# Two batches of attention share their tile shapes on TensorE, and row maxima are turned by a DMA that ScalarE issues

## The reference, cut to what matters

```python
def _mhsa(x, w_qkv, b_qkv, w_o, b_o):          # 8 heads of 64 channels
    t = x.reshape(B, C, H * W).transpose(0, 2, 1)
    q, k, v = jnp.split(t @ w_qkv + b_qkv, 3, axis=-1)
    q, k, v = (heads(q), heads(k), heads(v))
    scores = jnp.einsum('bhnd,bhmd->bhnm', q, k) / jnp.sqrt(jnp.float32(hd))
    attn = jax.nn.softmax(scores, axis=-1)
    out = jnp.einsum('bhnm,bhmd->bhnd', attn, v)
    return out.transpose(0, 2, 1, 3).reshape(B, H * W, C) @ w_o + b_o
...
hyp_out = _logmap0(_mhsa(_expmap0(x * m), hdn_w_qkv, ...))
euc_out = _mhsa(x * (1.0 - m), eu_w_qkv, ...)
return x + hyp_out + euc_out                    # x in the calls is _gn(x)
```

## Time and profile before

| | |
|---|---|
| median of 3 runs | 4022.13 us (4021.23 to 4025.07) |
| the profiled execution | 4021.88 us, its span 4020.2 us, mean granted clock 0.998 |
| busy, share of the span | PE 98%, PE weight loads 59%, DVE 58%, ACT 48%, POOL 66% |
| chain that ended last | PE 94%, DVE 2%, POOL 1%, DMA 1% |

### The profile page before, as it was taken

How to read it: one execution, slowest core, us unless ns; L and a number is a source line. 1 busy time by engine, 2 the same in 40 slices (tenths; PEclk the granted TensorE clock), 3 DMA queues, 4 the chain that set the end, 5 groups by cost and what they waited for, 6 DMA issues and landing times.

```text
span 4020.2 us, 57048 instructions
## 1 busy us (share of the span) xinstructions
PE 3937.1 (98%) x21664; PEld 2379.5 (59%) x21664; DVE 2345.5 (58%) x2553; ACT 1928.7 (48%) x3489; POOL 2664.2 (66%) x1303
## 2 busy tenths in 40 slices
PE   4999999999999999999999999999999999999998
PEld 3556566565655656556565665656556565565654
DVE  5464755647556475565746557465674656646455
ACT  4454534545345453555535545354553545535443
POOL 4584875838667486674857658675685756858468
PEclk9999999999999999999999999999999999999999
DMA  8212031121311213112141120411113121121101
GB/s 277 100 42 95 32 116 58 43 95 32 124 50 48 95 32 126 53 48 90 32 135 49 48 79 32 142 48 68 53 47 127 48 74 48 56 96 44 58 11 64
DMA packets 137548, 293.12 MB, mean 73 GB/s; under 512 B 16704, under 2 KB 28992, under 8 KB 127296
## 3 DMA queue, kind: packets, MB, share of 16 engines
q1 hardware_dynamic: 137280, 289.47, 21.2%
HBM read 239.09 MB, written 50.33 MB: 72 GB/s over the span
## 4 chain that ended last, share of the span: by engine, by line
PE 94%; DVE 2%; POOL 1%; DMA 1%; issue 1%; ACT 1%; SPq 0%; POOLq 0%; DVEq 0%; ACTq 0%
PE aux_ps L1310 32%; PE acc_ps L1422 23%; PE score_ps L1408 22%; PE aux_ps L1359 8%; PE score_ps L1310 4%; PE aux_ps L1432 3%; DVE mxp L1173 1%; PE aux_ps L1369 1%; POOL sums L673 1%; DMA w_split<-v_y 0%; DMA w_split<-w_o 0%; DMA xin<-in_x_dram 0%; PE aux_ps L1328 0%; PE aux_ps L1325 0%; POOL w_o L653 0%
## 5 line engine op out<-in xcount | busy, mean ns | idle before, releaser
L673 POOL TENSOR_TENSOR sums<-sums,probs 128x1024 f32<-128x1024 f32 x768 | 1835.4, 2390 | 736.9 <-ACT probs L850 682.6
L1173 DVE TENSOR_REDUCE mxp<-aux_ps 128x2 f32<-128x1024 f32 x1014 | 1241.7, 1225 | 1299.9 <-PE aux_ps L1359 1291.5
L850 ACT ACTIVATE probs<-score_ps 128x512 f32<-128x512 f32 x2048 | 1058.1, 602 | 658.7 <-PE score_ps L1408 648.0
L1422 PE MATMUL acc_ps<-probs,v_y 128*64 128x512 f32 x4096 | 991.9, 605 | 0.0
L1310 PE MATMUL aux_ps<-xs,w_qk 128*128 128x512 f32 x2976 | 804.7, 408 | 0.0
L1310 PEld LDWEIGHTS aux_ps<-xs,w_qk 128*128 128x128 f32 x2976 | 524.8, 188 | 374.3 <-issue 279.1
L673 POOL TENSOR_TENSOR sums<-probs 128x1024 f32<-128x1024 f32 x128 | 305.0, 2383 | 432.8 <-ACT probs L850 432.1
L1422 PEld LDWEIGHTS acc_ps<-probs,v_y 128*64 128x64 f32 x4096 | 248.2, 136 | 475.2 <-issue 245.2
L1359 PE MATMUL aux_ps<-k_hi,q_hi 64*128 64x512 f32 x2028 | 454.0, 443 | 18.7 <-DVE mxp L1173 16.1
L1235 DVE RECIPROCAL den<-den 128x256 f32<-128x256 f32 (+1 forms) x240 | 443.4, 1848 | 17.3 <-ACT den L861 17.3
L1408 PE MATMUL score_ps<-q_hi,k_hi 64*128 64x512 f32 x2048 | 407.9, 393 | 1.0 <-issue 1.0
(11 more groups left out here) (142 smaller groups left out, 3195.2 us busy)
## 6 DMA issues: line engine op xcount, KB each, us to landing
w_qk<-w_split SPq DMA_DIRECT2D x124, 512.0 KB, 4.2
xin<-in_x_dram SPq DMA_DIRECT2D x232, 256.0 KB, 3.3
w_o<-w_split SPq DMA_DIRECT2D x32, 1024.0 KB, 7.3
w_v<-w_split SPq DMA_DIRECT2D x30, 1024.0 KB, 5.9
v_y<-in_x_dram SPq DMA_DIRECT2D x72, 256.0 KB, 3.0
y<-v_y SPq DMA_DIRECT2D x64, 256.0 KB, 2.0
xin<-y SPq DMA_DIRECT2D x64, 256.0 KB, 2.9
out_dram<-v_y SPq DMA_DIRECT2D x64, 256.0 KB, 6.5
```

Of the source, the lines that this page charges most:

```text
L673: pool.tensor_tensor(sums[h][:, :], a, probs[:, g % SLOTS_P, :], ALU.add).then_inc(c_sum[h].sem, 1)
L850: act.activation(probs[:, n % SLOTS_P, token_half(u % 2)], score_ps[:, u % SCORE_BANKS, :], ACT.Exp, scale=SCALE).then_inc(c_exp.sem, 1)
L1173: dve.tensor_reduce(mxp[:, :, n, h], ps, AX.X, ALU.max).then_inc(c_free["D"].sem, 1)
L1422: last = nc.tensor.matmul(acc_ps[head(j), :], v_y[:, m, head(2 * p + j)], probs[:, n % SLOTS_P, token_half(j)], start=(m == 0), stop=(m == ...
```

## The change

Four things, besides renumbered waits for constants at the start:
- A projection is made whole, in one batch, always an even one (`QK_AT` is unchanged and even); of v, four tiles are made in batch 0 and four in batch 2. A gate tile goes between the two halves of such a projection.
- Probs x v is left out in even batches that have a projection; the odd batch does it for the batch before and for its own (`held`), with a due denominator between the two. The last two tiles fall in batch 31.
- The maxima are no longer turned on PE. DVE combines them in two halves (after slots 11 and 15), and ACT issues a DMA that stores a half to DRAM piece by piece (128 partitions x 8 values of 4 bytes) and, one batch later, a DMA that loads it as two rows of 512 into rows 0 and 64 of `q_max`. The load waits for the store to land; PE waits for the load before the first scores of each half. The identity matrix goes.
- In ACT's batch the denominator copy and `project` move to the end, behind these DMAs. On SP the load of `w_o` moves behind the chunks of the image.

```diff
+HALF_DONE = (11, 15)
+NEG_STORE, NEG_LOAD = (-3, -1), (-2, 0)
...
+def neg_at(b, what):
+    for h in range(2):
+        p, r = divmod(b - what[h], 8)
+        if r == 0 and 1 <= p <= PAIRS:
+            return p, h
+    return None
...
-    out = [("v", m) for m in (2 * b, 2 * b + 1) if m < NT]
+    out = [("v", m) for m in range(2 * b, 2 * b + 4) if b % 2 == 0 and m < NT]
     for p in range(2, PAIRS + 2):
-        for k in range(4):
-            done = min(8 * p + QK_AT[k], BATCHES)
-            first = done if (p, k) in ((PAIRS, 0), (PAIRS + 1, 3)) else done - 1
-            out += [("qk", p, k, part) for part in range(2) if b == (first, done)[part]]
+        out += [("qk", p, k) for k in range(4) if b == min(8 * p + QK_AT[k], BATCHES)]
     return out
...
+def held(i, t, b):
+    if projects(i, t, b - b % 2):
+        return (b - 1, b) if b % 2 else ()
+    return (b - 1, b) if b == BATCHES - 1 else (b - 1,) if b % 2 or not projects(i, t, b - 2) else ()
...
+            def store_neg(i, t, p, h):
+                n = 0 if i is None else 4 * t + p
+                act.wait_ge(c_mx.sem, c_mx.at(i, h + 1 if i is None else 2 * (n - 1) + h + 1))
+                if i is not None:
+                    act.wait_ge(c_neg[h].sem, c_neg[h].at(i, 16 * (n - 1)))
+                act.dma_start(max_dram[h].rearrange("j (n q) -> q (j n)", q=P),
+                              mxw[:, h, :, :].bitcast(F32).rearrange("p j n -> p (j n)")).then_inc(c_mst[h].sem, 16)
+            def load_neg(i, t, p, h):
+                act.wait_ge(c_mst[h].sem, c_mst[h].at(i, 16 if i is None else 16 * (4 * t + p)))
...
+                act.dma_start(q_max[0:HD + 1:HD, p % 2, token_half(h)].bitcast(F32), max_dram[h]).then_inc(c_neg[h].sem, 16)
...
 @@ ScalarE @@
                    for b in range(BATCHES):
                         for g in (2 * b, 2 * b + 1):
                             exps(g)
                         if phase_at(b, DRAIN) is not None:
                             drain(phase_at(b, DRAIN))
-                        if phase_at(b, DEN) is not None:
-                            den_copy(phase_at(b, DEN))
-                        if neg_pair(b) is not None and wanted(i, t, neg_pair(b)):
-                            neg_rows(i, t, neg_pair(b))
                         for j in HI_AT.get(b, ()):
                             if wanted(i, t, PAIRS):
                                 operand_hi(i, t, j)
-                        project(b)
...
                         operand_step(i, t, b)
+                        neg_turn(b)
+                        if phase_at(b, DEN) is not None:
+                            den_copy(phase_at(b, DEN))
+                        project(b)
...
@@ VectorE @@
+            def combine(i, t, p, h):
+                aux_read(dve, i, (t, "max", p, HALF_DONE[h]))
+                if i is not None:
+                    dve.wait_ge(c_mst[h].sem, c_mst[h].at(i, 16 * (4 * t + p - 1)))
+                dve.tensor_reduce(mxw[:, h, :, :], mxp[:, :, 4 * h:4 * h + 4, :], AX.X, ALU.max,
+                                  negate=True).then_inc(c_mx.sem, 1)
...
 @@ TensorE @@
                        scores(2 * b + 1)
                         if wanted(i, t, p1):
                             max_slot(i, t, p1, s1)
-                        if b:
-                            prob_v(2 * b - 2)
-                            prob_v(2 * b - 1)
-                        if phase_at(b, DEN) is not None:
-                            denominator(phase_at(b, DEN))
-                        if neg_pair(b) is not None and wanted(i, t, neg_pair(b)):
-                            neg_rows(i, t, neg_pair(b))
-                        if t == 0 and b in GATE_BATCH and followed(i):
-                            gate_tile(i, t, GATE_BATCH[b])
+                        for bb in held(i, t, b):
+                            prob_v(2 * bb)
+                            prob_v(2 * bb + 1)
+                            if phase_at(b, DEN) is not None and bb == b - 1:
+                                denominator(phase_at(b, DEN))
                         project(b)
-                    prob_v(TILES - 2)
-                    prob_v(TILES - 1)
```

More of the change, by code:

```diff
@@ L179, in aux_tiles @@
                 out += [((t, what, pp, k), "D", (first, first + 1))]
-        return out + neg(p) + maxima(p + 1, 0)
+        return out + maxima(PAIRS + 1, 0)
     out = []
@@ L187, in aux_tiles @@
             out += [((t, "den", phase_at(b, DEN)), "A", (1,))]
-        if neg_pair(b) is not None and wanted(i, t, neg_pair(b)):
-            out += neg(neg_pair(b))
         if t == 0 and b in GATE_BATCH and followed(i):
             out += [((t, GATE_BATCH[b]), "D", (0,))]
-        for f in projections(b):
+        for f in projections(b) if b < BATCHES else ():
             if f[0] == "v":
-                out += [((t,) + f, "A", (LAST_SCORE if f[1] % 2 else 1 if f[1] == 6 else 2,))]
-            elif f[3] and wanted(i, t, f[1]):
-                out += [((t,) + f[:3], "Q", (2,))]
+                out += [((t,) + f, "A", (LAST_SCORE if f[1] % 2 else 2,))]
+            elif wanted(i, t, f[1]):
+                out += [((t,) + f, "Q", (2,))]
     if wanted(i, t, PAIRS + 1):
@@ L334, in build @@
         c_mx = counted("max_made", 16, 2)
+        c_mst = [counted(f"max_stored{h}", 16 * 8, 16) for h in range(2)]
+        c_neg = [counted(f"max_rows_loaded{h}", 16 * 8, 16) for h in range(2)]
         c_score = counted("scores_made", NSC)
@@ L577, in _ @@
                         load_chunks(i, 1, "norm", range(4, 8), next_image)
+                    load_wide(w_o, t, 6, c_wo)
                     sp.wait_ge(c_aux.sem, c_aux.at(i, at(i, (t, "v", NT - 1))[1] + 1))
@@ L616, in _ @@
                 sp.wait_ge(c.sem, 17 + B * 128 - 16 * PAIRS + 16)
+            for c in (*c_mst, *c_neg):
+                sp.wait_ge(c.sem, 17 + B * 128 - 16)
             sp.wait_ge(c_wv.sem, 1 + B * 64 - 32)
@@ L784, in qk_hi @@
                                bias=bias_q[:, tt, what, pp:pp + 1]).then_inc(c_hi.sem, 1)
[L786 to L790, removed]
+            def store_neg(i, t, p, h):
[7 more added lines that the diff above has]
+                act.wait_ge(c_mst[h].sem, c_mst[h].at(i, 16 if i is None else 16 * (4 * t + p)))
+                last = TILES * t + 16 * (p - 2) + 8 * h + 8
+                if i is not None and (i or last > 0):
+                    act.wait_ge(c_score.sem, c_score.at(i, 2 * last))
+                act.dma_start(q_max[0:HD + 1:HD, p % 2, token_half(h)].bitcast(F32), max_dram[h]).then_inc(c_neg[h].sem, 16)
             def split_hi(n):
@@ L877, in project @@
                     def project(b):
-                        for f in made(b):
+                        for f in projections(b):
                             if f[0] == "v":
@@ L882, in project, with neg_turn @@
                                 qk_hi(i, t, f[1], f[2])
+                    def neg_turn(b):
+                        if b == 0 and t:
+                            load_neg(i, 0, PAIRS, 1)
+                        elif b == 0 and i:
+                            load_neg(i - 1, 1, PAIRS, 1)
+                        elif neg_at(b, NEG_LOAD) and wanted(i, t, neg_at(b, NEG_LOAD)[0]):
+                            load_neg(i, t, *neg_at(b, NEG_LOAD))
+                        if neg_at(b, NEG_STORE) and wanted(i, t, neg_at(b, NEG_STORE)[0]):
+                            store_neg(i, t, *neg_at(b, NEG_STORE))
                     for b in range(BATCHES):
@@ L1361, in max_slot @@
                 last.then_inc(c_aux.sem, 1)
-            def neg_rows(i, t, p):
-                pe.wait_ge(c_mx.sem, c_mx.at(i, 2 if t < 0 else 2 * (4 * t + p)))
-                for h in range(2):
-                    ps = bank_free(pe, i, (t, "neg", p, h))
-                    for n in range(4):
-                        last = nc.tensor.matmul(ps[0:HD + 1, n * P:(n + 1) * P], mxw[:, 4 * h + n:4 * h + n + HD + 1],
-                                                ident[:, :], start=True, stop=True)
-                    last.then_inc(c_aux.sem, 1)
             for g in GATES:
@@ L1453, in project @@
                     def project(b):
+                        gate = GATE_BATCH[b] if t == 0 and b in GATE_BATCH and followed(i) else None
                         for f in projections(b):
```

78 lines of the change are left out of this document (30 added, 48 removed).

## The result

The changed kernel was not 2.4% faster, as forecast (3924 us), but about 1% slower. Two of its four runs fell to a granted clock of 0.616 and 0.670 and took 5748 and 5305 us (the plain median of the four is 4687.65); their cause is open, and they are left out here. The other two took 4059.43 and 4070.32 us, the kernel before 4021.23 to 4025.07 beside them; ratio 1.0105 (95% interval 1.0087 to 1.0124). The profiled execution is the one of 4059.43 us, span 4057.7.

A forecast was written before the change was run, and what follows sets the result against it. The prediction took PE, busy 98% of the span, as the bound: 116 us saved on PE, less 15 for DVE and 3 for the start, is 98, so 3924 us from 4022; range 3898 to 3974 (8 in 10).

The forecast's parts named there:

- The store's landing: ACT's store of half the maxima to DRAM: lands in some 4 us, hidden, costs nothing; 13 kept for the range.
- rival A: Slow store holds ACT's load, high halves and exps: 110 places per microsecond, gain gone at 9.4 us; slower, chance 0.07.
- The cover: Between ACT's store and load: a landing up to 9 us is hidden, 8 for the second half.
- The page's rule: Skill page on DMA receipts and writes under 512 B: would mean a slow store; by the rows it costs nothing.
- Merges: Joined PE runs: two Q runs of 6 into 12 save 0.24 us, two V runs of 8 into 16 save 0.15.
- Rival C: On PE, joined runs gain nothing, only the turned maxima do: 30 us less 3, 3995 us; chance 0.04.
- The sum of 116 us: PE's list shortened by joined projections and probs x v and turned maxima, less new neighbours: 116 us, at worst 93.
- the turn: Turning row maxima by DMA takes 0.47 us net off PE each time, 63 times: 30 us.
- DVE, 15 us: Shorter even batches make PE wait for DVE to read max tiles: 15 us lost, bounds 0 and 64.
- Rival B: DVE makes PE wait for max tiles in nearly every fourth batch: 60 us instead of 15, 3969 us; chance 0.13.
- The start, 3 us: First maxima stored and loaded by DMA among 1 MB transfers before the first scores: 3 us lost, bounds -1 and 8.
- the worst neighbours: Q runs on PE behind a max tile instead of V: at worst 23 us less gain, giving 3945 us.

The follow-up runs named there:

- the two sets of runs: The changed kernel measured twice, unaltered: first mean 4064.9 us (ratio 1.0105), then once more beside the other experiments 3997.02 us (ratio 0.9939).
- the best kernel: Changed kernel with stores in 32-byte runs, loads gathering, and only the very first maxima turned on PE with the identity: 3900.62 us, ratio 0.9699.
- the two halves of the pairing: Against the kernel before, maxima turned on PE: only projections made whole, 4201.25 us; only probs x v paired (v by four tiles), 4202.96 us.
- the second and fourth experiment: Second: kernel before with only the turn by DMA, 4091.92 us. Fourth: changed kernel with each load one batch later, slow store kept, 3939.32 us.
- the repeat: The changed kernel, unaltered, measured once more on the same chip as other experiments: 3997.02 us, ratio 0.9939.

## Why the prediction was wrong, step by step

- **The store's landing, the step that failed.** "I take the row of the small pieces, some 4 us, so nothing": it took 10.3 to 11.0 in the median, 18.4 and 15.4 at the start. The row chosen was a load of small pieces from DRAM; no row of before showed small stores to it. Both ends were in the text (3.7 and 13), and the choice between them decided the sign. This was rival A, with a chance of 0.07 for "slower", far too low for an operation that no row showed, with a cover of 9 us inside its bounds; and the 13 us that were kept "for the range" are in none of its numbers (3898 to 3974). What rival A said of the place held: ACT's load holds the projections' rounding. Its price, 110 us for a microsecond, came near the 91 of the two sets of runs in part by luck, as said there. Its point of decision was a little early: 9.4 us, where the changed kernel at 10.3 is still 25 us faster than before.
- **The cover.** 9 us were worked out, some 10.8 found, and that is two errors that partly cancel. The store was issued 2.6 us into its odd batch (522.22 with the first max tile at 519.61; 2.6 is also the median of the 126 later stores), not 5.0: in the timeline the issue stands before the batch's last exp. But the deadline wasn't the exps' 6.95 + 5.49 + 1.47 + 1.5 less 1.3 = 14.1. PE's second max tile comes sooner, at 6.95 + 5.49 + 0.43 + 1.84 = 14.7, less 0.7 for the rounding, 0.5 for the load's issue and 0.1 for semaphores: 13.4. 13.4 - 2.6 = 10.8 us are an estimate from these rows; the landing shown had 10.9. Without the denominator it is 0.86 less.
- **The clock.** The prediction counted a wait as its length. After the longer ones PE also worked at 1.2 GHz: 41 us of the 142 by which the changed kernel's span exceeds the one with 32-byte stores are PE's busy time, with the mean granted clock at 0.989 and 0.996. By these means the clock makes some 29 of the 41 (4057.7 x 0.011 - 3915.3 x 0.004, an estimate); the rest isn't traced.
- **The page's rule.** "DMA: Bandwidth & Descriptors" of the Trainium skill (Anatomy of one DMA, written for DMAs that GpSimd issues) warned of a surprisingly long delay of the receipt when the target is HBM; its Specifications say that below 512 B a DMA does read-modify-write. The runs agree with the first, for a DMA that ScalarE issued: the store is slow after its data have moved, below. But the second rule doesn't separate the cases: pieces of 32 B land in 1.4 us and pieces of 4 B, 64 B apart, in 2.7, all of them far under 512 B. The same page's Rules for kernel authors advise to make the last dimension contiguous. The edit that repaired it does so for the store, and undoes it for the load; spacing the values 64 B apart, against that advice, did nearly as well.
- **Merges.** Q 2.95 to 2.96 (2.96 forecast), V 3.58 to 3.59 (3.59), V with denominator 1.87 + 0.86 + 1.72 = 4.45 (4.45). Right. Rival C is out.
- **The sum of 116 us.** With the store repaired and the start as before, the kernel gains 4021.78 - 3900.62 = 121.2. Right within 5 us. How near it came is in part luck, since its parts sit less well. Alone, the turn gave 21 of 30 us. In the pairs it gave 3956.14 - 3900.62 = 55.5, most of it, as I read it, because there the turn stood inside a joined V run: 63 x (0.63 + 0.15) = 49. And the new order without it gave 66 where 86 less 63 x 0.15 = 77 were to be had; the missing 11 aren't explained.
- **DVE, 15 us.** Wrong, though harmless: in the best kernel PE waits for max tiles 10.9 us in 21 waits, in the one before 16.1 in 26. Rival B is out. But the mechanism is real, as the two halves of the pairing show: it bites at batches of 4.1 to 4.4 us, hardly at 5.49.
- **The start, 3 us.** Mis-sized. With 32-byte stores it costs 3916.77 - 3900.62 = 16.2 us in the total, 8.1 of them before the first probs x v. PE's waits for max tiles over the span are 10.3 us longer as well (21.2 against 10.9), I don't know why; with the changed kernel's own, 25.3 (138.9 - 113.6). I had counted 3.7 us for a landing; in the crowded start even the quick store takes 7.18 and its load 8.56, and the slow one 18.36.
- **The result put together.** 4064.9 - 3900.6 = 164 us stand between the best version and the changed kernel: 25 at the start, 139 at some 126 later landings, 1.1 us for each on average, waits and lower clock together.
- **A slip.** The upper end of the forecast's own range adds 23 us for the worst neighbours to 3924, which makes 3947 and not 3945; nothing hangs on it.

What stays open: the 11 us of the new order, and the 9 that the turn alone lacks in place.

## What to carry to other kernels

An operation that no row of the profile shows, placed ahead of others on an engine in order, is to be given the chance that its bounds have, not that of the nearest row: compare its cover (here 9 to 11 us) with both ends before the sum is made. A transposing store of single values to DRAM should be made contiguous on the DRAM side, and the load should do the gathering; and the wait for it belongs as late in the in-order engine's list as its reader allows. When batches are shortened by moving work to their neighbours, look at the shortest batch that results: what counts is whether every engine that frees banks still gets through in it.

## What the runs showed of the hardware

**The time of such a store passes after its data have moved.** The DMA view of 521 to 536 us of the changed kernel, 40 slices of 0.375 us (busy tenths of the DMA engines):

```profile
DMA  0000027200000000000000000000000000000106
```

The store issued at 522.22 keeps the engines busy from slice 6 to 8, until 524.0; it lands at 533.81. For 9.8 us nothing moves that the profile shows. Values 64 bytes apart land about four times sooner, though the queue moves more packets in all (264448 against 133632, since the load gathers too).

**Such a landing isn't steady** from one set of runs to another: 0.7 us in the median for the same kernel (11.0 and 10.3; 10.2 and 10.1 for the same store in the second and fourth experiment), with 0.6% faster in one set and 1% slower in the other, while the medians of the kernel before in the four sets lie within 0.02% (4021.78 to 4022.31). A kernel whose path holds such a landing can't be judged by one set.

**Small pieces cost much less when they are read than when they are written side by side**: the load that gathers 1024 values of 4 bytes lands in 4.8 us (my median from the semaphores' records), the store of as many in 10 to 11; 64 bytes apart the store took 2.7 to 3.5, less than the load.

**PE's granted clock falls after some of its longer waits.** 0.50 from 696 to 700 us of the changed kernel, behind a wait of 3.09 us, and 1.00 again by 702; 48 us at that level between 140 and 3880 us, 14 in the repeat, none in the kernel before or with 32-byte stores.
